# A four-layer graph network on one core: three accumulation tables instead of two, the degree count in pairs of tiles, the first layer norm on ScalarE

## The reference

```
def _edge_norm(edge_index, num_ent):                  # layer 0
    deg = segment_sum(ones, row, num_ent)             # row = src
    deg_inv = where(deg > 0, rsqrt(maximum(deg, 1.0)), 0.0)
    return deg_inv[row] * deg_inv[col]
out = segment_sum((x[dst] @ W) * norm[:, None], src)  # sums go to the unsorted end

h = maximum(layernorm(x), 0.0); x = x + L0(h, ...)    # degree-normalised sum
h = maximum(layernorm(x), 0.0); x = x + L1(h, ...)    # edge network, sum by dst, gates
h = maximum(layernorm(x), 0.0); x = x + L2(h, ...)    # sum of neighbours, two matmuls
h = maximum(layernorm(x), 0.0); x = x + L3(h, ...)    # mean of neighbours, two matmuls
```

## Time and profile before

| what | value |
|---|---|
| median of three runs | 10491.45 us |
| the profiled execution | 10494.6 us |
| its span, first to last instruction | 10492.8 us |
| first and last issue of the layer 0 scatter (L664) | 441.5 and 3763.7 us |
| first gather of layer 1 (L862) | 3881.5 us |
| granted TensorE clock, mean | 0.635 of full speed |

### The profile page before, as it was taken

The page is one execution under the profiler, slowest core; times in us unless marked ns, Lnnn a source line. Parts: engine busy times, 40 slices in busy tenths (PEclk is TensorE's granted clock), DMA queues, the critical chain, the costliest instruction groups (busy, mean ns, idle before and its releaser), DMA issues. The chain is left out here.

```text
span 10492.8 us, 125271 instructions
## 1 busy us (share of the span) xinstructions
PE 5872.1 (56%) x34164; PEld 5377.4 (51%) x34165; DVE 3273.7 (31%) x5018; ACT 566.7 (5%) x1060; POOL 7489.8 (71%) x6808
## 2 busy tenths in 40 slices
PE   8655555555555558888888843333333533333334
PEld 5455555555555548888778733333333433333334
DVE  7633333333333334333333331111111211111111
ACT  0000000000000010000000110000000100000000
POOL 0277777777777757777777667777777377777776
PEclk9855555555555567777777766555555566556655
DMA  1133333333333342222222111111111111111111
GB/s 48 19 19 19 18 19 19 18 19 19 19 18 18 19 68 44 43 43 43 43 43 43 32 32 26 26 26 27 26 26 26 27 27 27 26 26 26 26 27 34
DMA packets 671521, 303.55 MB, mean 29 GB/s; under 512 B 580273, under 2 KB 584219, under 8 KB 671211
## 3 DMA queue, kind: packets, MB, share of 16 engines
q0 software_dynamic: 399360, 218.53, 17.9%
q1 hardware_dynamic: 270663, 83.75, 3.5%
q10 hardware_dynamic: 1444, 0.62, 0.0%
HBM read 220.48 MB, written 81.91 MB: 29 GB/s over the span
## 5 line engine op out<-in xcount | busy, mean ns | idle before, releaser
L862 POOL DMA_INDIRECT h_rows<-h_tab,idx x3328 | 3179.2, 955 | 1157.5 <-issue 936.1
L664 POOL DMA_INDIRECT part<-total,row_at x1664 | 2585.3, 1554 | 1172.9 <-issue 725.9
L1414 PE MATMUL ps_seg<-hot,h_rows 128*64 128x128 f32 x6656 | 1497.3, 419 | 2586.4 <-DMA h_rows<-h_tab,idx 2505.8
L1414 PEld LDWEIGHTS ps_seg<-hot,h_rows 128*64 128x64 f32 x6656 | 1353.0, 226 | 2718.5 <-issue 1948.9
L862 POOL DMA_INDIRECT a_rows<-a_tab,idx x1664 | 1589.8, 955 | 536.4 <-issue 506.6
L1343 DVE TENSOR_TENSOR acc_t<-acc_t,ps_seg 64x128 f32 x416 | 116.5, 280 | 2903.3 <-PE ps_seg L1414 2903.3
L576 PE MATMUL ps_dst<-identb,relb 128*128 128x128 bf16 x1672 | 216.4, 311 | 1365.5 <-DVE relb L512 1365.5
L576 PEld LDWEIGHTS ps_dst<-identb,relb 128*128 128x128 bf16 x1672 | 161.6, 141 | 1401.6 <-DVE relb L512 1398.6
L1034 PE MATMUL ps_seg<-hot,act_rows 128*65 128x128 f32 x3328 | 666.4, 383 | 320.5 <-ACT act_rows L1107 320.1
L1034 PEld LDWEIGHTS ps_seg<-hot,act_rows 128*65 128x65 f32 x3328 | 598.8, 205 | 345.3 <-issue 340.8
L592 PE MATMUL ps_tot<-msg,same 128*128 128x64 f32 x3328 | 647.3, 376 | 99.0 <-issue 99.0
(11 more groups left out here) (172 smaller groups left out, 6089.9 us busy)
## 6 DMA issues: line engine op xcount, KB each, us to landing
h_rows<-h_tab,idx POOLq DMA_INDIRECT x3328
edge<-edge_t SPq DMA_DIRECT2D x208, 132.0 KB
part<-total,row_at POOLq DMA_INDIRECT x1664, 3.2
a_rows<-a_tab,idx POOLq DMA_INDIRECT x1664
idx<-src_steps SPq DMA_DIRECT2D x624, 4.0 KB, 1.5
part<-acc_t SPq DMA_DIRECT2D x2, 3360.0 KB
u_win<-u_tab SPq DMA_DIRECT2D x208, 32.0 KB
b_win<-b_tab SPq DMA_DIRECT2D x208, 32.0 KB, 2.2
```

The costliest lines, as they stand in the source:

```text
L664: pool.indirect_dma_start(parts[k % PARTS][:, :], bass.IndirectOffsetOnAxis(ap=row_at[:, b, k:k + 1], axis=0), total[:, b, k, :], None, co ...
L862: pool.indirect_dma_start(dest[:, r, k, :], None, table[:, :], bass.IndirectOffsetOnAxis(ap=idx[:, r, k:k + 1], axis=0)).then_inc(landed[r ...
L1414: last = pe.matmul(ps_seg[0:F, b, 0, :], rows_of[:, r, k, :], hot[:, b, k, :], start=(k == 0), stop=(k == K - 1))
```

## The change

- `PARTS` is 3. The tables are one tensor `parts_tab` of 3 x 13440 rows, and the table of a tile goes by its number mod 3: a copy of the source numbers, `srcf_at`, has 0, 13440 or 26880 added and replaces `srcf` in `row_at`. The scatter waits for the landing three issues back.
- The count takes 16 tiles at a time (`UT`), 104 units. The one-hots are laid out as pairs of tiles, `[P, 8, 128, 2]` and `[P, 8, 98, 2]`, so neighbouring elements of a matmul operand lie 2 apart (4 bytes), and `one_hi` has 98 columns instead of 104. VectorE makes the codes of the first 448 tiles, starts the count, and does the other codes and the windows in three pauses of the count.
- The casts `dstf`, `srcf`, `spare`, `src_hi`, `srcf_at` and four small memsets move from VectorE to GpSimd.
- The first layer norm of x is done by ScalarE column by column during the count: 104 copies with a sum, 104 subtractions of the mean, 104 squares with a sum, one root. After the count VectorE multiplies the norm's factor with `dinv` and does one pass over h in four chunks. The scan rows come after that. SyncE no longer waits for `u_tab` before the barrier, but at the start of the next stage.
- A third table is zeroed, and loaded back in part 3. There GpSimd adds three tables by two dependent additions, and the addition to x moves to VectorE. The centre and variance steps of the norm stand one group earlier.
- In all later norms the squares go to two buffers of 34 columns in place of one of 104, and `square` waits for the `variance` two chunks back.

```diff
-PARTS = 2
+PARTS = 3
+PART_ROWS = NP + P
...
-        parts = [nc.dram_tensor(f"part{k}", [NP + P, F], F32).ap() for k in range(PARTS)]
+        parts_tab = nc.dram_tensor("parts_tab", [PARTS * PART_ROWS, F], F32).ap()
+        parts = [parts_tab[k * PART_ROWS:(k + 1) * PART_ROWS, :] for k in range(PARTS)]
...
-            one_lo = sb(ph, "one_lo", [P, 2, P, K], BF16)
-            one_hi = sb(ph, "one_hi", [P, 2, J, K], BF16)
-            iota_k = sb(ph, "iota_k", [P, P, K], BF16)
+            one_lo = sb(ph, "one_lo", [P, 2, K, P, 2], BF16)
+            one_hi = sb(ph, "one_hi", [P, 2, K, JU, 2], BF16)
+            iota_k = sb(ph, "iota_k", [P, P, 2], BF16)
...
+                    pool.wait_ge(dst_in, 16)
+                    pool.tensor_copy(dstf[:, 0:TILES], cols_i[:, 1, :]).then_inc(dstf_ready, 1)
+                    pool.wait_ge(src_in, 16)
+                    pool.tensor_copy(srcf[:, :], cols_i[:, 0, :]).then_inc(srcf_ready, 1)
+                    pool.wait_ge(srcf_ready, 1)
+                    for k in range(PARTS):
+                        pool.tensor_scalar(srcf_at[:, k:TILES:PARTS], srcf[:, k:TILES:PARTS], float(k * PART_ROWS),
+                                           None, ALU.add).then_inc(pool_coded, 1)
+                    pool.wait_ge(spare_row_ready, 1)
+                    pool.tensor_scalar(spare[:, :], srcf[:, :], -1.0, spare_row[:, 0:1], ALU.mult,
+                                       ALU.add).then_inc(pool_coded, 1)
+                    pool.wait_ge(his_coded, 2)
+                    pool.tensor_scalar(src_hi[:, 0:TILES], hi_b[:, :], float(P), None, ALU.mult).then_inc(pool_coded, 1)
...
+                    act.wait_ge(x_loaded, 16)
+                    for j in range(J):
+                        nc.scalar.activation(h_nm[:, j, :], x_nm[:, j, :], ACT.Copy,
+                                             accum_out=stat[:, 0, j:j + 1]).then_inc(summed, 1)
...
+                    for j in range(J):
+                        nc.scalar.activation(h_nm[:, j, :], x_nm[:, j, :], ACT.Identity,
+                                             bias=stat[:, 1, j:j + 1]).then_inc(x_centered, 1)
...
+                    for j in range(J):
+                        if j >= 4:
+                            act.wait_ge(x_squared, j - 3)
+                        nc.scalar.activation(dump[:, j % 4, :], h_nm[:, j, :], ACT.Square,
+                                             accum_out=stat[:, 2, j:j + 1]).then_inc(x_squared, 1)
...
+                                hold(dve, counted, u - 1)
+                                dve.tensor_tensor(one_lo[:, b, :, :, :], iota_k[:, None, :, :].to_broadcast([P, K, P, 2]),
+                                                  src_lo[:, tiles].rearrange("p (q k) -> p q k", k=2)[:, :, None, :]
+                                                  .to_broadcast([P, K, P, 2]), ALU.is_equal).then_inc(los, 1)
...
+                                for q in range(K):
+                                    for k in range(2):
+                                        last = pe.matmul(ps_deg[:, 0:JU], one_lo[:, b, q, :, k], one_hi[:, b, q, :, k],
+                                                         start=False, stop=False, skip_group_check=True)
+                                last.then_inc(counted, 1)
...
+                    sp.wait_ge(table_stored, 16 * CHUNKS)
...
-                            dve.tensor_tensor(row_at[:, b, :], ndup[:, 1, :], srcf[:, tiles], ALU.add).then_inc(at_ready, 1)
+                            dve.tensor_tensor(row_at[:, b, :], ndup[:, 1, :], srcf_at[:, tiles], ALU.add).then_inc(at_ready, 1)
...
                                 pool.indirect_dma_start(
-                                    parts[k % PARTS][:, :], bass.IndirectOffsetOnAxis(ap=row_at[:, b, k:k + 1], axis=0),
+                                    parts_tab[:, :], bass.IndirectOffsetOnAxis(ap=row_at[:, b, k:k + 1], axis=0),
                                     total[:, b, k, :], None, compute_op=ALU.add).then_inc(slot_done[b][k], 16)
...
                         pool.tensor_tensor(agg[:, g % 3, :, :], sums[0][:, cols, :], sums[1][:, cols, :],
+                                           ALU.add).then_inc(pair_added, 1)
+                        pool.wait_ge(pair_added, g + 1)
+                        pool.tensor_tensor(agg[:, g % 3, :, :], agg[:, g % 3, :, :], sums[2][:, cols, :],
                                            ALU.add).then_inc(agg_ready, 1)
```

More of the change, by code:

```diff
@@ L148, in gnn_kernel, with __init__ @@
         class Norm:
-            def __init__(self, c, turn, scale=None, smalls_before=0, bounds=None):
-                self.sq = sb(c, f"sq_{turn}", [P, J, F])
+            def __init__(self, c, turn, smalls_before, bounds):
+                self.sq = sb(c, f"sq_{turn}", [P, 2, J // 3, F])
                 self.st = sb(c, f"st_{turn}", [P, 5, J])
-                self.scale = scale
-                self.chunks_before = turn * CHUNKS
+                self.chunks_before = (turn - 1) * CHUNKS
                 self.smalls = smalls_before
-                bounds = bounds or [c * JC for c in range(CHUNKS + 1)]
                 self.chunks = [slice(bounds[c], bounds[c + 1]) for c in range(CHUNKS)]
@@ L183, in rescale @@
                 self.small(dve, dve.reciprocal(st[:, 1, cc], st[:, 4, cc]))
-                if self.scale is not None:
-                    self.small(dve, dve.tensor_tensor(st[:, 1, cc], st[:, 1, cc], self.scale[:, cc], ALU.mult))
                 dve.scalar_tensor_tensor(out=h_nm[:, cc, :], in0=h_nm[:, cc, :], scalar=0.0,
@@ L188, in rescale @@
                                          op1=ALU.mult).then_inc(normed, 1)
-            def vector(self, dve):
-                for part in (self.center, self.variance, self.rescale):
-                    for c in range(CHUNKS):
-                        part(dve, c)
             def square(self, act, c):
@@ L258, in _ @@
                                      acc_t[:, 0:(J + 1) * F]).then_inc(zeroed, 16)
-                    norm.store(sp, u_tab, 0)
+                    for c, end in enumerate(ends):
+                        cc = slice(ends[c - 1] if c else 0, end)
+                        sp.wait_ge(normed, c + 1)
+                        sp.dma_start(by_node(u_tab)[:, cc, :], h_nm[:, cc, :]).then_inc(table_stored, 16)
                     sp.wait_ge(zeroed, 16 * PARTS)
@@ L371, in _ @@
                         step(dve.tensor_copy(meta[:, half], ps_b[0:1, 2, c * P:c * P + HALF]))
-                    settled()
+                    dve.wait_ge(x_rooted, 1)
+                    step(dve.reciprocal(stat[:, 4, :], stat[:, 3, :]))
+                    dve.wait_ge(counted, UNITS)
+                    step(dve.tensor_scalar(deg[:, 0, :], ps_deg[:, 0:J], 1.0, None, ALU.max))
+                    step(dve.tensor_scalar(deg[:, 1, :], ps_deg[:, 0:J], 0.0, None, ALU.is_gt))
+                    settled()
+                    dve.sem_inc(deg_ready, 1)
+                    dve.wait_ge(deg_rooted, 1)
+                    step(dve.reciprocal(dinv[:, :], deg[:, 2, :]))
+                    settled()
+                    step(dve.tensor_tensor(dinv[:, :], dinv[:, :], deg[:, 1, :], ALU.mult))
+                    settled()
+                    step(dve.tensor_tensor(stat[:, 4, :], stat[:, 4, :], dinv[:, :], ALU.mult))
+                    settled()
+                    dve.wait_ge(x_centered, J)
+                    for c, end in enumerate(ends):
+                        first = ends[c - 1] if c else 0
+                        dve.scalar_tensor_tensor(out=h_nm[:, first:end, :], in0=h_nm[:, first:end, :], scalar=0.0,
+                                                 in1=stat[:, 4, first:end, None].to_broadcast([P, end - first, F]),
+                                                 op0=ALU.max, op1=ALU.mult).then_inc(normed, 1)
                     step(dve.tensor_tensor_scan(rows[:, 1, :], rows[:, 0, :], rows[:, 0, :], 0.0, ALU.add, ALU.bypass))
@@ L411, in _ @@
                     last.then_inc(ranges_turned, 1)
[L413 to L423 removed]
+                    count(SECOND, THIRD)
                     pe.wait_ge(range_cols, 1)
@@ L431, in _ @@
                     last.then_inc(ranges_spread, 1)
+                    count(THIRD, TURNS2)
                     pe.wait_ge(b2_negated, 1)
@@ L670, in gnn_kernel @@
         end_stage()
+        early.close()
         with ExitStack() as ph:
@@ L676, in gnn_kernel @@
             ends = (7, 14, 20, GROUPS)
-            sums = [acc_t[:, k * J * F:(k + 1) * J * F].rearrange("p (j f) -> p j f", f=F) for k in range(PARTS)]
-            norm = Norm(ph, 1, smalls_before=5 * CHUNKS, bounds=[0] + [e * JG for e in ends])
+            sums = [acc_t[:, k * J * F:(k + 1) * J * F].rearrange("p (j f) -> p j f", f=F) for k in range(2)]
+            sums.append(sb(ph, "sum2", [P, J, F])[:, :, :])
+            norm = Norm(ph, 1, smalls_before=0 * CHUNKS, bounds=[0] + [e * JG for e in ends])
             agg = sb(ph, "agg", [P, 3, JG, F])
```

(4 more changed lines are left out.)

190 lines of the change are left out of this document (103 added, 87 removed).

## The result

The changed kernel took 10065.8 us (median of four runs, 10058.88 to 10070.23) against 10491.92 us (10488.84 to 10494.59) for the kernel before on the same chip: ratio 0.9593, 95% interval 0.9581 to 0.9605. It is faster by 426 us; the forecast was 310 us (10182), and the range from 10150 on did not reach down to it.

| part | before | after | change | forecast |
|---|---|---|---|---|
| start to the first scatter issue | 441.5 | 275.8 | -165.7 | -147 |
| first to last scatter issue | 3322.2 | 3069.0 | -253.2 | -170 |
| last scatter issue to first gather of layer 1 | 117.8 | 120.4 | +2.6 | +8 |
| first gather of layer 1 to the end | 6611.3 | 6591.8 | -19.5 | 0 |

What follows compares the result with a forecast made beforehand. GpSimd was read as busiest, with landings two back also setting the scatter's pace and a TensorE-VectorE ring the count's. 10494.6 - 147 (front and count) - 170 (scatter) + 8 (update) = 10185.6, median 10182 us; own range 10150 to 10235, 8 in 10: 10150 to 10280.

Steps and rivals of the forecast that it cites:

- which two terms are large: whole kernel: first scatter issue 147 us earlier, and the scatter stage 170 us shorter.
- forecast 9 + 8: count: 9 us for work put into its pauses, plus 8 us on the path for GpSimd's casts.
- excluded one another: front: GpSimd's memset and VectorE's cast did so; the same expected of GpSimd's casts, 5 to 17 us.
- Some long gaps stay, since no landing causes them: scatter: gaps over 1 us outlast the removed wait; 70 us allowed, 240 us gained instead of 170 if none stays.
- The count's term: count: 104 units at 2.22 us each, 231 us in all, bounds 224 and 291.
- 256 columns ... so 0.095 us: count: a load and multiply pair of 226 columns takes 0.095 us, scaled from 256 columns in 0.11 us.
- The ring of the earlier trace: count before: loads 1.33, release 0.67, VectorE's turn 1.31 make 3.31 us per two steps, 344 us for 208.
- the lower bound that I gave (VectorE never waits): count: VectorE alone sets the pace, 2.15 us per unit, 224 us.
- the first rival: count: TensorE's pairs stay at 0.166 us or its clock halves and it bounds the ring; 60 to 86 us lost; chance 0.12.
- VectorE kept its rate: count: VectorE forecast at 0.55 ns per element; the rival on its rate had chance 0.04.
- the scatter did not stay at 1.998: scatter rival: pace unchanged because something other than landings holds it; 170 us more, 10352; chance 0.08.
- the issue on GpSimd got no dearer: scatter rival: longer table or third transfer makes issues dearer, each 0.1 us costing 166 us; chance 0.04.

Runs made afterwards that it cites:

- experiment 11: changed kernel, but GpSimd makes srcf, srcf_at, spare and src_hi only after the count; 10051.6 us in one run.
- experiment 1: changed kernel with its three tables, but each scatter issue waits for the landing two back; 11679.8 us against 11871.5 for the kernel before, ratio 0.9838.
- experiment 2: changed kernel with two tables in one tensor, so the wait is two back; ratio 0.9827 to the kernel before.
- experiment 3: changed kernel with two tables as two tensors of their own, wait two back; ratio 0.9826 to the kernel before.
- experiment 5: kernel before, unchanged, on another chip for a second trace; 11778.0 us in one run.
- experiment 10: kernel before with 6656 bytes of unused memory ahead of the layer 0 stage's small tiles; 10491.6 us, ratio 1.0001.
- experiment 9: kernel before with four scatter tables and the wait four back, update still adding two; 10261.1 us against 10491.7, ratio 0.9781.
- experiment 6: changed kernel, unchanged, on a chip where the kernel before is slower; 11376.0 us against 11769.0, ratio 0.9664.

## Why the prediction was right and where it failed

**Right:** the direction, which two terms are large, and that landings two back set the scatter's pace. Also the tail: 4.6 us from the degree to the first store (240.20 to 244.79), 18.3 to the first window (263.04), 12.8 to the first issue, forecast 13. The pauses and what GpSimd's casts cost VectorE are together 240.2 - 13.1 - 104 x 2.021 = 16.9 us, forecast 9 + 8, but this is luck in part: without the casts (experiment 11) it is 232.6 - 11.1 - 210.2 = 11.3, so the pauses took 2.3 more and the casts, 5.6 in the count, 2.4 less. That the memset and VectorE's cast "excluded one another" was my reading of one row: in the trace of before VectorE's cast of 5.96 us ends at 7.15 us, 0.08 after GpSimd's memset (1.38 + 5.69). The casts don't show it in that strength: VectorE lost 7.6 us to 16.7 us of them (experiment 11).

**The step that failed: "Some long gaps stay, since no landing causes them".** I read the label "issue" of the earlier trace rows as proof that the gaps don't hang on the wait, and added 70 us; but 725.9 us of the earlier trace rows carry that label, with those that I put down to landings among them. The gaps do hang on the wait. In the trace of before, 1170 of the 1558 issues with a recorded landing two back start 0.76 to 0.80 us after it. Of the 37 issues with such a landing and a gap over 1 us ahead of them, 18 start 1.34 to 1.36 us after it and 16 start 1.96 us after it, with the landing on time (one more follows a late landing, of 4.8 us, and two start 1.44 us after theirs).

They aren't scattered. Counted from 0, issues 113, 211, 309 and so on to 1583, every 98th, start 1.96 us after the landing, all 16 of them; issues 60, 105, 150 to 1635, every 45th, start 1.35 us after it (two of them 1.44), all 33 whose landing is recorded. Of the 39 gaps over 1 us, 38 belong to these two series, and the last is that of the late landing. The earlier trace rows shows issues 780, 799 and 825. Every kernel here that waits two back has the long delays at these same issue numbers, on each chip, whatever else differs (experiments 1, 2, 3, 5 and 10). In the changed kernel the same issues start 0.30 us after the end of the one before, like all others. An example, issues 111 to 113 in the timeline of before:

```profile
663.50 1.55 POOL L664 DMA_INDIRECT part<-total,row_at  x1 [0.47 <-issue]
665.42 1.55 POOL L664 DMA_INDIRECT part<-total,row_at  x1 [0.37 <-issue]
668.58 1.55 POOL L664 DMA_INDIRECT part<-total,row_at  x1 [1.60 <-issue]
```

The line's own view, cut to the issue at 663.50 alone, has its landing:

```profile
DMA to landing us min/median/max: 3.1/3.1/3.1
```

It landed at 666.6, and the next but one started 1.96 us later. So a gap takes both: one of these places in the count of issues, and an engine that is still waiting for a landing there. An engine that finds its semaphore already there has none (0.30 us at the same issues in the changed kernel and in experiment 9). Experiments 1 to 3 bring the gaps back with the wait, experiment 9 takes them away from the kernel before. With 70 us of gaps left out and 1.8578 for 1.853, the wait is worth 170 + 70 - 8 = 232, as measured in experiment 9, and within the bound of 240 that I gave for it. Of the 70 only 46 were there: so much do the two series stand above 0.30 us (26 and 20 us). What adds 0.6 us at every 45th issue and 1.2 at every 98th was not tried and stays open.

**The other part of the scatter, 21 us:** an issue takes 1540 ns in the changed kernel and all its variants (1538 to 1541), 1553 or 1554 in the kernel before and both its variants, on each chip. 1664 x 12.9 ns (the means 1553.6 and 1540.7) = 21.5 us; 232 + 21.5 = 253. The gathers of identical code are 4.6 ns shorter (means 955.3 and 950.7), 4992 x 4.6 = 23 us. GpSimd sets the pace of these three stages on the first chip, each gather starts 0.305 us after the one before has ended, and the stages are 7.5, 7.3 and 7.4 us shorter, 22 in all. The updates and the end between and behind them take 3 us more: together the 19.5 us that I forecast as 0. The shorter durations don't come from the chip (experiments 5 and 6), the tensors (3), the wait (1, 9) or the tiles' addresses in that stage (10). What in the rest of the kernel does it stays open.

**The count's term was mis-sized, 231 for 210 us, in the step "256 columns ... so 0.095 us".** I read the earlier trace rows as load and multiply one after the other, 128 + 128 columns in 0.11 us at full clock. The records of the changed kernel have a load beside the multiply before it: the multiply that starts at 119.46 us lasts 0.21 (its end is modelled), the next load starts at 119.50. A multiply of 98 columns follows the last after 0.046 us at full clock and after 0.081 at a granted 0.50. The granted clock at 2010 us, where the earlier trace rows stand, is 0.50 as well, and there a multiply of 128 columns follows the last after 0.106 us. That fits the multiply's columns alone (0.081 x 128 / 98 = 0.106); with the load's 128 columns added it would be 0.081 x 256 / 226 = 0.092. The mean of 0.57 of that stage should have told me of the clock. The old pair was misread too: 1.33 / 8 is not the distance of two pairs, since the first two loads of the row stand 0.04 us apart; in the trace the multiplies of that unit start 0.19 us apart, 1.53 us for 8. The ring of the earlier trace rows came out right all the same, because what I took too little for TensorE I had in the 0.67 us behind it. With this TensorE needs 0.8 or 1.3 us a unit, not 1.5; the lower bound that I gave (VectorE never waits) was the right case, and it measured 2.02 a unit instead of 2.15, since VectorE's two operations follow at 1.13 + 0.89. Against that stands a later start, 13.1 instead of 10: I counted the cost of GpSimd's casts in the count but not in the codes (2 us of it go with the casts of experiment 11). Together -20.8 + 3.1, so the first issue came 18 us before its forecast.

**The rivals.** TensorE's clock did fall (0.59) as the first rival had it, but the part that says TensorE then bounds the ring didn't follow. VectorE kept its rate (from start to start 1.13 us for 2048 elements, where 1024 had 0.61), the scatter did not stay at 1.998, and the issue on GpSimd got no dearer.

**The update.** +2.6 where I had +8. The loads came as thought: GpSimd's first addition stands 24.8 us after the last issue, 20.5 before:

```profile
3369.58 0.72 POOL L795 TENSOR_TENSOR agg<-acc_t 128x256 f32<-128x256 f32 x1 [23.24 <-DMA sum<-parts_tab]
```

The third table costs 13 to 15 us by experiments 1 to 3, not 8, and I had no gain for the moved addition and the earlier norm steps, which give 9 to 11 together; which of them gives it was not tried. ScalarE's norm took 73 us where I allowed 140, hidden either way.

## What to carry to other kernels

When a queue of transfers is held by a completion some places back, price the removal of that wait with the smallest idle time (0.30 us here), and count the long gaps as part of the wait too if they end at fixed distances after a completion (1.35 and 1.96 us here), whatever the label on the idle time says. Number the instructions as well: gaps that look scattered in time stood here at every 45th and every 98th issue. Operands of TensorE whose neighbours lie 16 bytes apart cost here four times those 4 bytes apart (0.18 us a pair against 0.046, both at full clock), so test an operand's layout by itself before pricing a stage with it, and read the clock of the stretch beside any row that is carried over. Once one engine binds a stage, as VectorE did the count, work on others can be free unless it holds that engine up: the norm on ScalarE cost nothing, GpSimd's casts 7 us.

## What was not expected of the hardware

- A GpSimd that waits for a landing starts 0.77 us after it, but at every 45th issue 1.35 us and at every 98th 1.96 us after it, at the same issue numbers in every kernel with that wait. Where nothing is waited for, the same issues have the 0.30 us of all others.
- A pair of weight load (128 columns) and multiply (98 columns) follows the last after 0.046 us with a step of 4 bytes and after 0.18 with one of 16, both at full clock.
- Indirect DMA issues on GpSimd of the same code differ by up to 6 ns (means of gathers 951 to 957) and by 13 ns (scatters) from kernel to kernel. The scatters' 13 ns are the same on each chip, the gathers of one kernel move by up to 2 ns between chips. From the kernel before to the changed one it is 44 us over 6656 issues, more than some of the edits are worth.
- One program took 10490 us on one chip and 11770 to 11870 us on others, with nearly all of the difference in the edge stages of layers 1 to 3. TensorE's granted clock is lower there (0.64 against 0.75 in the first, 0.57 against 0.59 in the others), but the last two give half of the difference with TensorE busy a third of the time, so the clock alone is not shown to be the cause.
